# Edges of a graph layer sorted in 50 chunks of 2,000, with one record scatter a chunk, in place of 40 chunks of 2,500 with a pair of scatters for two chunks

## The reference, cut to what matters

```python
support  = layernorm(x) @ W.T + bias                  # 6250 x 256
messages = support[dst] * edge_weight[:, None]        # 100000 edges
x = x + segment_sum(messages, src, 6250)
x = x + lstm_block(layernorm(x))                      # 256 wide, over 6250 rows, then a gated prefix and suffix sum
```

## Time and profile before

| | us |
|---|---|
| median of 3 runs | 1592.95 |
| lowest and highest | 1589.33, 1593.96 |
| the profiled execution's own time | 1597.74 |
| span of its trace | 1595.9 |
| build of the first chunk of portion A begins | 138.14 |
| load of the first portion's records begins | 252.56 |
| first gather of portion B | 258.93 |
| load of the other records begins | 594.10 |

### The profile page before, as it was taken

How to read it: one execution, slowest core, us unless ns; L and a number is a source line. 1 busy time by engine, 2 the same in 40 slices (tenths; PEclk the granted TensorE clock), 3 DMA queues, 4 the chain that set the end, 5 groups by cost and what they waited for, 6 DMA issues and landing times.

```text
span 1595.9 us, 36211 instructions
## 1 busy us (share of the span) xinstructions
PE 1386.4 (87%) x9451; PEld 1226.0 (77%) x9451; DVE 1318.6 (83%) x4072; ACT 637.3 (40%) x2150; POOL 1024.3 (64%) x1087
## 2 busy tenths in 40 slices
PE   5688784777878876999999999999999999999991
PEld 2457784666666653899999999999999988999990
DVE  8799886999999977888888888888888745666665
ACT  0525660000000000444444444444444477777770
POOL 0225645777777777777777776777777400888883
PEclk9799986989999987999999999999999999999995
DMA  9111102333433333444444443444444444433435
GB/s 237 51 40 52 31 12 58 95 87 92 139 86 96 89 93 100 132 144 142 153 132 153 126 154 122 154 128 154 125 152 127 142 131 120 128 119 119 127 93 162
DMA packets 60867, 183.27 MB, mean 115 GB/s; under 512 B 20474, under 2 KB 22050, under 8 KB 59810
## 3 DMA queue, kind: packets, MB, share of 16 engines
q0 software_dynamic: 41312, 98.34, 22.3%
q1 hardware_dynamic: 19500, 84.30, 16.7%
HBM read 141.25 MB, written 41.17 MB: 114 GB/s over the span
## 4 chain that ended last, share of the span: by engine, by line
PE 60%; DVE 11%; issue 6%; DVEq 2%; POOL 1%; ACT 1%; DMA 1%; ACTq 0%; POOLq 0%
PE bank L2015 14%; PE bank L1965 13%; PE bank L2009 11%; PE bank L2002 8%; PE bank L1917 6%; PE bank L1880 5%; DVE big_a L1233 3%; DVE big_b L1481 1%; PE bank L1984 1%; PE bank L1975 1%; DVEq L1297 1%; DVE big_a L1694 1%; DVE big_c L1440 1%; DVE big_a L1228 1%; POOL big_a L586 1%
## 5 line engine op out<-in xcount | busy, mean ns | idle before, releaser
L633 POOL DMA_INDIRECT big_a<-support_scratch,stg_g x510 | 486.9, 955 | 172.1 <-issue 141.8
L1965 PE MATMUL bank<-big_a,big_c 128*125 128x256 f32 x1020 | 306.1, 391 | 15.7 <-issue 4.5
L586 POOL DMA_INDIRECT big_a<-support_scratch,stg_g x224 | 213.8, 954 | 75.8 <-issue 57.2
L2015 PE MATMUL bank<-big_c 128*128 128x125 f32 x2048 | 256.8, 281 | 4.6 <-DVE big_c L1453 3.4
L2015 PEld LDWEIGHTS bank<-big_c 128*128 128x128 f32 x2048 | 241.3, 191 | 15.4 <-issue 7.1
L1481 DVE TENSOR_TENSOR big_b<-big_b,bank 125x256 f32 x510 | 212.5, 417 | 41.0 <-PE bank L1965 38.5
L1565 DVE TENSOR_SCALAR big_c<-consts_sb,listed 128x125 f32<-128x125 f32 x510 | 188.9, 371 | 46.9 <-PE bank L1965 42.6
L2002 PEld LDWEIGHTS bank<-xt,w_ih 128*128 128x128 f32 x1600 | 209.1, 192 | 11.1 <-ACT xt L696 0.7
L2009 PEld LDWEIGHTS bank<-big_c 128*128 128x128 f32 x1600 | 209.1, 192 | 10.9 <-ACT bank L810 0.4
L2002 PE MATMUL bank<-xt,w_ih 128*128 128x125 f32 x1600 | 209.5, 275 | 0.5 <-ACT xt L696 0.5
L2009 PE MATMUL bank<-big_c 128*128 128x125 f32 x1600 | 209.9, 275 | 0.0
(11 more groups left out here) (308 smaller groups left out, 2320.2 us busy)
## 6 DMA issues: line engine op xcount, KB each, us to landing
big_c<-gate_input_scratch SPq DMA_DIRECT2D x64, 508.0 KB, 3.5
gate_input_scratch<-pr SPq DMA_DIRECT2D x25, 1016.0 KB, 4.3
big_a<-support_scratch,stg_g POOLq DMA_INDIRECT x734
support_scratch<-pr SPq DMA_DIRECT2D x12, 448.0 KB
big_b<-in_x SPq DMA_DIRECT2D x2, 1904.0 KB
out<-big_a SPq DMA_DIRECT2D x2, 1456.0 KB
big_b<-in_x SPq DMA_DIRECT2D x1, 1792.0 KB
out<-big_a SPq DMA_DIRECT2D x1, 1344.0 KB
```

Source lines behind the costliest of these rows:

```text
L586: pool.indirect_dma_start(out=ring[:, s, :], out_offset=None, in_=sup_d, in_offset=bass.IndirectOffsetOnAxis(ap=stg_g[:, q, j:j + 1], axis ...
L633: pool.indirect_dma_start(out=ring[:, s, :], out_offset=None, in_=sup_d, in_offset=bass.IndirectOffsetOnAxis(ap=stg_g[:, r, n:n + 1], axis ...
L1965: mm(bank[4 + POSITION[n] % PSR][0:SEGS, 0:D], oneh[:, s % HELD, 0:SEGS], ring[:, s, :], start=True, stop=True).then_inc(prod, 1)
L2015: return mm(home, w_hh[:, k, g:g + P], h_s[:, q, k, :], start=False, stop=True, skip_group_check=True)
```

## The change

- `CC` goes from 20 to 16 and so `CHUNKS` from 40 to 50. Each chunk is sorted by itself to 128 blocks of 32: the one-hot of the line is 32 wide, a matmul of `permute` has 64 columns to stream and not 128, there are 16 of them a chunk (800 in all, as before), and each chunk has one scatter. A scatter waits until the one before it has landed.
- The constants and small operations that dealt with pairs go (`number_i`, `both`, `half`, `grp_i`), and one check for over 128 blocks comes.
- `PORTIONS` goes from (14, 26) to (18, 32), and with it the first gather portion from 224 to 232 tiles; the 510 tiles behind it stay. The hottest chunks kept apart go from 4 to 5 (10,000 edges both times).
- In portion A ScalarE makes the slot one-hot of every third chunk (6 of 18), with two buffers. The block rows are computed for five chunks at a time, so ten times and not four, five of them inside portion B.
- During ranking there are 25 support projections and not 20, behind it 3 and not 8.
- Portion B is written out tile by tile on all engines: a chunk every 7 tiles (`SPACING`), the scatter of chunk i of the portion behind gather 7(i+3)-1, and the last three scatters behind the last gather, ahead of `load_records(1)`.
- The ten ring slots of a place are exchanged between even and odd places.

```diff
-CC = 20
+CC = 16
-PORTIONS = (14, 26)
+PORTIONS = (18, 32)
-NPOS = GRP * BLK
+SIDES = CHUNKS // SIDE
+SPREADS = 4
+MASKED = (0, 5, 10, 15, 20, 25, 30, 35, 40, 43, 48, CHUNKS)
-SOON, FORE, RANKING, MID = 7, 14, 20, 8
+SOON, FORE, RANKING, MID = 7, 14, 25, 3
+SPACING = 7
-ROWS_AT = {2: 2, 3: 6}
+ROWS_IN_A = {3: 1, 7: 2, 11: 3, 15: 4}
+ROWS_IN_B = {5: 5, 9: 6, 14: 7, 18: 8, 23: 9}
...
+        def chunk_at(t):
+            return t // SPACING if t % SPACING == 0 and t // SPACING < PORTIONS[1] else None
+        def by_scalar(k):
+            return k < K0 and k % 3 == 2
...
-            def add_blocks(m, q, rows):
-                pool.wait_ge(evac, m + 3)
-                if not isinstance(m, int) or m > 0:
-                    pool.wait_ge(scat, scattered(m))
-                pool.sem_inc(go, 1)
-                for g in range(GRP):
-                    pool.indirect_dma_start(
-                        out=rec_d, out_offset=bass.IndirectOffsetOnAxis(ap=rows(g), axis=0),
-                        in_=stg_r[:, q, g, :], in_offset=None, compute_op=ALU.add).then_inc(scat, 16)
+            def add_blocks(k, rows):
+                pool.wait_ge(evac, k + 3)
+                if k > 0:
+                    pool.wait_ge(scat, scattered(k))
+                pool.indirect_dma_start(
+                    out=rec_d, out_offset=bass.IndirectOffsetOnAxis(ap=rows, axis=0),
+                    in_=stg_r[:, k % 2, :], in_offset=None, compute_op=ALU.add).then_inc(scat, 16)
...
+            def gather(t):
+                hh, j = t // HALF, t % HALF
+                if j == 0:
+                    pool.wait_ge(gst, hh + 1)
+                pool.wait_ge(prod, t + RING - LOOK_1)
+                pool.indirect_dma_start(
+                    out=ring[:, t % RING, :], out_offset=None, in_=sup_d,
+                    in_offset=bass.IndirectOffsetOnAxis(ap=stg_g[:, hh % 2, j:j + 1], axis=0)).then_inc(gat[t % RING], 16)
...
-            with pool.Fori(1, whole) as it:
-                for q in range(2):
-                    gather_half(0, it * 2 + q, q, HALF)
-                second_portion(it + (M0 - 1))
+            for t in range(TIL[0]):
+                gather(t)
+                i = chunk_at(t + 1)
+                if i is not None and i >= 3:
+                    second_portion(K0 + i - 3)
+            for i in range((TIL[0]) // SPACING - 2 if TIL[0] // SPACING < PORTIONS[1] else PORTIONS[1] - 3, PORTIONS[1]):
+                second_portion(K0 + i)
             load_records(1)
...
-                V.tensor_tensor(col_h, c.broadcast_to([EP, CC, NPOS]), several(iota[0:EP, 0:NPOS], CC), ALU.is_equal
+                V.tensor_tensor(col_h, c.broadcast_to([EP, CC, BLK]), several(iota[0:EP, 0:BLK], CC), ALU.is_equal
...
-            with dve.Fori(begin, whole) as it:
-                builds_and_tiles(it)
+            for t in range(TIL[0]):
+                i = chunk_at(t)
+                if i is not None:
+                    build(K0 + i)
+                    if i in ROWS_IN_B:
+                        spread_blocks(ROWS_IN_B[i])
+                        rows_of_blocks(ROWS_IN_B[i])
+                if t % HALF == 0:
+                    vals = blocks(t, HALF)
+                if t + AHEAD < TIL[0]:
+                    onehot(t + AHEAD, t + AHEAD)
+                add_tile(t, t, acc[0:SEGS, ds(vals[t % HALF], D)])
...
                 for c in range(CC):
-                    ins = mm(bank[b][:, 0:2 * NPOS], slots_home(k, q)[:, c, :],
-                             col_v[:, q, c, :, :].rearrange("p v n -> p (v n)"),
-                             start=q == 0 and c == 0, stop=q == 1 and c == CC - 1)
+                    ins = mm(bank[b][:, 0:2 * BLK], slots_home(k)[:, c, :],
+                             col_v[:, k % 2, c, :, :].rearrange("p v n -> p (v n)"), start=c == 0, stop=c == CC - 1)
```

More of the change, by code:

```diff
@@ L107, in build @@
         ident, iota, before, shift, ones = (consts[:, i, :] for i in range(5))
[L108 to L112, removed]
+        chunk_c = sb("chunk_consts", [CHUNKS, 3 * CHUNKS + 5 + 2 * BB])
+        earlier, first, cold = (chunk_c[:, i * CHUNKS:(i + 1) * CHUNKS] for i in range(3))
+        first_p, blocks_n, cold_p, hot_p, over = (chunk_c[:, 3 * CHUNKS + i:3 * CHUNKS + i + 1] for i in range(5))
+        hot_at, hot_n = (chunk_c[:, 3 * CHUNKS + 5 + i * BB:3 * CHUNKS + 5 + (i + 1) * BB] for i in range(2))
         leader = ident[0:CHUNKS, 0:2]
-        block_no = sb("block_no", [P, GRP])
+        block_no = sb("block_no", [P, 1])
         rank_b = sb("rank_b", [P, P], bf16)
@@ L571, in _ @@
                 finish_support(t)
[L572 to L588, removed]
+            for k in range(K0):
+                pool.wait_ge(where_r, k // SIDE + 1)
+                add_blocks(k, where_b[:, k:k + 1])
+                if EARLY + k < NB:
+                    finish_support(EARLY + k)
+            def gather(t):
[6 more added lines that the diff above has]
+                    in_offset=bass.IndirectOffsetOnAxis(ap=stg_g[:, hh % 2, j:j + 1], axis=0)).then_inc(gat[t % RING], 16)
             def load_records(p):
                 pool.wait_ge(table_t, 1)
-                pool.wait_ge(scat, scattered(sum(PORTIONS[:p + 1]) // 2))
+                pool.wait_ge(scat, scattered(sum(PORTIONS[:p + 1])))
                 if p > 0:
@@ L763, in stage_values @@
+            def stage_values(k):
                 act.wait_ge(built, k - 1)
[L764 to L769, removed]
[L770 to L771 removed]
@@ L792, in _ @@
-            stage_rows(whole + M0 - 1)
-            act.wait_ge(prod, whole * RING + RING)
-            stage_gather(whole * RING + HALF, 1, TIL[0] - whole * RING - HALF)
+            for i in range(2):
+                stage_values(K0 + i)
+            act.wait_ge(where_r, SIDE)
+            for t in range(1, TIL[0]):
+                if t % HALF == 0 and t // HALF >= 2:
+                    stage_half(t // HALF)
+                i = chunk_at(t)
+                if i is not None:
+                    if i + 1 < PORTIONS[1] and i >= 1:
+                        stage_values(K0 + i + 1)
+                    if i >= 2:
+                        copy_records(K0 + i - 2)
+                        stage_rows(K0 + i - 2)
@@ L796, in take_input @@
+            for i in range(PORTIONS[1] - 2, PORTIONS[1]):
+                copy_records(K0 + i)
+                stage_rows(K0 + i)
             def take_input(j, q, x, free=None):
@@ L996, in _ @@
             dve.wait_ge(iota_r, 1)
-            wide = [EP, SIDE, BB, CC]
-            for k in range(0, CHUNKS, SIDE):
+            for k, end in zip(MASKED, MASKED[1:]):
+                wide = [EP, end - k, BB, CC]
                 V.tensor_tensor(
-                    mask(k, SIDE),
-                    bk[:, k * CC:(k + SIDE) * CC].rearrange("p (k o c) -> p k o c", o=1, c=CC).broadcast_to(wide),
+                    mask(k, end - k),
+                    bk[:, k * CC:end * CC].rearrange("p (k o c) -> p k o c", o=1, c=CC).broadcast_to(wide),
                     place_iota[0:EP, :, :].rearrange("p (o b) c -> p o b c", o=1).broadcast_to(wide),
@@ L1313, in _ @@
             unpack_all(0)
-            for i in range(2, SUPERS // SIDE):
-                spread_blocks(i)
             dve.wait_ge(small_r, 1)
@@ L1907, in _ @@
             pe.sem_inc(prod, RING)
-            for k in range(PORTIONS[0]):
-                permute(k, k % 2, k // 2 + 1, k // 2 % 2)
+            for k in range(K0):
+                permute(k, k + 1, k % 2)
+                if k + 1 in ROWS_IN_A:
+                    blocks_of(ROWS_IN_A[k + 1])
                 if EARLY + k < NB:
```

319 lines of the change are left out of this document (127 added, 192 removed).

## The result

The changed kernel took 1630.53 us (median of four runs, 1625.93 to 1633.73), the kernel before 1593.45 beside it on the same chip (1589.33 to 1594.03). The ratio is 1.0233, with a 95% interval of 1.0212 to 1.0254: slower by 2.3%. The forecast was 1598.5, the range ended at 1611.

A forecast was written before the change was run, and what follows sets the result against it. The prediction saw VectorE and GpSimd full in portion B and no engine full in portion A. Preparation -1, portion A -16 and portion B +22.5 gave +5.5 us on 1592.95, about 1598.5 us; range 1582 to 1611.

The forecast's parts named there:

- Times 5.38 / 4.63 for the clock as portion A granted it, 87 us: Portion A: TensorE's 75 us of work at full clock, scaled by the clock of the kernel before, become 87 us.
- my 98: Portion A: takes 98 us, 16 less than 114.4, with bounds of 84 and 107 us.
- The price of a narrow matmul: Portion A, TensorE: a 64-column matmul behind 128-wide weights costs 0.21 us at full clock, between 0.116 and 0.2315.
- The columns halved thus give little: Portion A, TensorE: a chunk's permutation is 16 x 0.21 = 3.4 us at full clock, against 4.63 before.
- Rival 3: Portion B: TensorE's clock falls to 0.50 for a third of the chunks, some 9 us on top, 1608 us; chance 0.12.
- TensorE at half clock is all busy, and its clock came back in such stretches: Portion B: the argument against the rival in which TensorE's clock falls there and adds some 9 us.
- Portion B: Gathers and scatters: GpSimd alone becomes the bound, at 10.7 us a chunk; +22.5 us, bounds +18 and +30.
- The tail's scatters: End of portion B: three scatters behind the last gather, 3.4 us apart, have nothing to hide their landing, 4.5 us.
- Preparation: Ahead of portion A: address arithmetic 3 us earlier, ranking 2 us later; portion A's first build 1 us earlier.
- Scatters in portion A: GpSimd in portion A: scatters stay dear (2.29 us before) through SBUF interfaces shared with VectorE; their chain takes 90 us.
- Writing out: Portion B's loops written out: costs nothing, bounds 0 and a gain of 1 us on register work.
- Behind portion B: All behind 594 us: nothing changes in number, it only moves with portion B's end; difference 0.

The follow-up runs named there:

- wide columns: Changed kernel with each matmul of portion A's permutations streaming its 64 columns twice (128 columns): 1605.06 us, ratio to before 1.0076.
- the wide run: Changed kernel with 128 streamed columns in both portion A and portion B: 1605.74 us, ratio to before 1.0089.
- the extra gathers: Changed kernel with one more gather of 128 rows behind each scatter of portion B, 32 in all: 1666.14 us, ratio to before 1.0454.

## Why the prediction was wrong

- **The step that failed** is "Times 5.38 / 4.63 for the clock as portion A granted it, 87 us". That factor, 1.16, was carried over from a portion A with 128-column matmuls and ten projections. The changed kernel's matmuls are narrow and its projections end at 184 us, and the factor was 100.8 / 66 = 1.52. At 0.244 us a matmul I had 70 us for all permutations; they took 100.8. The difference, 31 us, is the miss of portion A (28.5) and more. With wide columns, where the clock is nearly as before, portion A took 102.6, against my 98.
- **The price of a narrow matmul** was put at 0.21 between bounds of 0.116 and 0.2315; it is 0.230, the upper bound. "The columns halved thus give little" was right in its direction; they give nothing. Worth 288 x 0.02 = 6 us at full clock. The estimate of 0.213 us from the Trainium skill (TensorE: Matmul & The Clock Gate, LDWEIGHTS), twice its time for a load of 128 weight columns, is 7% below the 0.230 of this trace.
- **The low clock was looked for in the wrong portion.** Rival 3 had it fall in portion B and make that 9 us longer. It fell there too, to 0.80, and cost nothing: the wide run gave 0.91 and the same B. The argument "TensorE at half clock is all busy, and its clock came back in such stretches" had been read off a kernel with wide matmuls, and it fails where narrow ones are nearly all that TensorE runs: all busy for 62 us, and no return.
- **Portion B**: +24.0 against +22.5. GpSimd's pitch, 1.25 and 1.9 us, VectorE's 83%, the idle time ahead of `add_tile` and the tail are as forecast; the extra gathers confirm the bound. The tail's scatters came 3.9 to 4.0 us apart, not 3.4, and cost 6.1 us more than hidden ones, not 4.5.
- **Preparation**: -5.9 against -1. The ranking pitch was 0.48. The kernels with the changed code that I traced begin portion A between 132.3 and 135.2, those with the code of before at 132.9, 133.4 and 138.1, so no gain of the change can be told here from one execution to the next. Since this one execution of before was late, the difference of the medians is larger than that of the spans. In the spans the misses of the stages, 28.5 + 1.5 - 4.9 - 0.2 - 2.3 = 22.6 us, make up the 22.7 between +5.5 and +28.2.
- **Scatters in portion A**: their median fell from 2.13 to 1.56 us with the changed kernel, and was 1.84 with wide columns. I had kept them dear by a rule of the Trainium skill (GPSIMD Engine Reference, the table of its properties). The traces agree in the main: in the changed kernel VectorE is idle more than half of the time from 190 us on, and the five scatters from 221.32 to 248.67 us, with no build beside them, took 1.54 us each; those of 174.02 and 190.48, with builds beside them nearly throughout, took 3.54 and 3.49. In the run with wide columns the scatter of 3.54 us from 215.37 lies beside the builds of 215.22 and 217.42. Yet the one at 183.99 of the changed kernel took 1.63 us with builds beside it throughout, so what sets the size is open.
- **Writing out** costed at nothing: 2.5 us of gain in the kernel before, more than the bound of 1 that I gave it, and small beside the miss.
- **Behind portion B** all versions of the changed kernel take 998.8 to 1000.0 us on the first chip, both of before 1001.4 to 1001.8. I did not look for the cause.

## What to carry to other kernels

A busy share of 100% says nothing without the granted clock beside it: carry over the price of an instruction, and the clock only if the mix of the engine's work stays the same. When an edit makes matmuls narrower, ask first whether width was what they cost; here 64 columns cost what 128 did, and streaming the same columns twice made the kernel 25 us faster because the clock stayed up. When an edit cuts work into more pieces, count the pieces on the engine that issues them, and let the last ones land under other work.

## What the runs showed that I had not expected

- TensorE stayed at a granted 0.51 for 64 us with 64.00 us of matmuls of 64 columns, and was at 0.93 to 1.00 in the same place with the same matmuls at 128 columns.
- An f32 matmul with 128-wide weights took 0.230 us at 64 columns and 3.74 / 16 = 0.234 at 128.
- An indirect scatter of 16 rows took 1.36 us on GpSimd, one of 128 rows 1.61.
- On two other chips of the same type the kernel before took 1962.51 and 1943.68 us in place of 1592. Portion A shows little of it (before's code, written out: 114.7 us on the second chip, 111.7 on the first). Portion B of the same two runs was 390.1 and 334.0, and what stands behind it 1301.7 and 1001.4: the 510 gathers there start over 956 us and over 657. So most of the difference lies in the stages with gathers. Why is open.
